# The one-hot of dst moves from VectorE (one comparison) to ScalarE (eight absolute differences and a relu)

## What is computed

```python
msg  = relu(x[src] + edge_attr @ We + be)              # 200000 x 128
aggr = segment_sum(msg, dst, num_segments=6250)
h = (1 + eps) * x + aggr
h = relu(h @ W1 + b1) @ W2 + b2
h = (h - mean(h)) * rsqrt(var(h) + 1e-5) * gamma + beta   # over the nodes
h = relu(h) + x
out = layernorm(x + h)                                  # per node
```

## Time and profile before

| | |
|---|---|
| time, median of 3 runs | 1583.06 us (1581.17 to 1585.45) |
| the profiled execution: span from its first to its last instruction | 2684.1 us; the page gives no other time of it |
| instructions in it | 58837 |
| TensorE busy | 1871.5 us, 70% of the span |
| GpSimd busy | 1154.5 us, 43% |
| VectorE busy | 991.5 us, 37% |
| ScalarE busy | 841.5 us, 31% |
| mean granted clock of TensorE | 0.809 of full speed |

### The profile page before, as it was taken

How to read it: one execution, slowest core, us unless ns; L and a number is a source line. 1 busy time by engine, 2 the same in 40 slices (tenths; PEclk the granted TensorE clock), 3 DMA queues, 4 the chain that set the end, 5 groups by cost and what they waited for, 6 DMA issues and landing times.

```text
span 2684.1 us, 58837 instructions
## 1 busy us (share of the span) xinstructions
PE 1871.5 (70%) x23395; PEld 1369.8 (51%) x23395; DVE 991.5 (37%) x3361; ACT 841.5 (31%) x1954; POOL 1154.5 (43%) x1193
## 2 busy tenths in 40 slices
PE   1776777776777777677767767767767776766776
PEld 0455555555555555555555555555555555555554
DVE  6433333333333333333333333333333333333335
ACT  3232323232332333232323323323223322322335
POOL 6444444444444444444444444434434444444421
PEclk9877788787887787788888778878778778887888
DMA  8222222232222222222222222222222222222221
GB/s 231 62 59 65 62 59 68 59 71 66 63 63 61 61 62 64 61 66 59 67 61 61 65 61 63 65 58 65 64 58 67 61 62 63 63 65 62 62 86 50
DMA packets 148455, 180.61 MB, mean 67 GB/s; under 512 B 41677, under 2 KB 128932, under 8 KB 147924
## 3 DMA queue, kind: packets, MB, share of 16 engines
q1 hardware_dynamic: 102489, 89.62, 14.0%
q0 software_dynamic: 37728, 77.31, 11.5%
q10 hardware_dynamic: 7963, 9.90, 1.2%
HBM read 170.09 MB, written 6.63 MB: 66 GB/s over the span
## 4 chain that ended last, share of the span: by engine, by line
PE 66%; issue 20%; another core or an unknown queue 8%; ACT 2%; DVE 1%; ACTq 0%; DVEq 0%
PE ps L1330 23%; PE ps L1315 15%; PE ps L1255 12%; PE ps L1269 11%; PE ps L1296 1%; PE ps L1276 1%; PE ps L1299 1%; ACT xg L694 1%; PE ps L1287 1%; PE ps L1384 1%; ACT slotS L680 0%; PE ps L1288 0%; PE ps L1394 0%; DVE lnst L1197 0%
## 5 line engine op out<-in xcount | busy, mean ns | idle before, releaser
L574 POOL DMA_INDIRECT xg<-xb,idxb x1145 | 1106.6, 966 | 1423.9 <-DVE msg L937 1068.8
L1330 PE MATMUL ps<-iota_all 128*128 128x128 bf16 x4032 | 377.8, 247 | 425.7 <-issue 291.3
L688 ACT ACTIVATE iota_all<-ps 128x384 bf16<-128x384 f32 x896 | 408.5, 489 | 775.6 <-remote 567.8
L1330 PEld LDWEIGHTS ps<-iota_all 128*128 128x128 bf16 x4032 | 290.1, 111 | 515.6 <-issue 511.5
L1022 DVE TENSOR_TENSOR accT<-accT,ps 128x64 f32 x390 | 86.5, 222 | 1138.4 <-remote 992.8
L1255 PE MATMUL ps<-we,ea 64*128 64x128 f32 x3126 | 344.2, 367 | 45.7 <-issue 45.3
L1330 PE MATMUL ps<-iota_all,hot_all 128*128 128x128 bf16 x4032 | 301.1, 229 | 102.6 <-issue 98.8
L937 DVE TENSOR_TENSOR msg<-ps,xg 128x512 f32<-128x512 f32 x390 | 262.0, 686 | 238.9 <-PE ps L1255 233.2
L1330 PEld LDWEIGHTS ps<-iota_all,hot_all 128*128 128x128 bf16 x4032 | 247.2, 102 | 172.4 <-issue 145.0
L1255 PEld LDWEIGHTS ps<-we,ea 64*128 64x128 f32 x3126 | 288.0, 261 | 80.7 <-issue 72.2
L1269 PE MATMUL ps<-msg,hot 128*64 128x128 f32 x3120 | 300.9, 352 | 6.2 <-issue 4.5
(11 more groups left out here) (135 smaller groups left out, 1113.8 us busy)
## 6 DMA issues: line engine op xcount, KB each, us to landing
ea<-in_eat SPq DMA_DIRECT2D x156, 320.0 KB
lowB<-lowD SPq DMA_DIRECT2D x128, 224.0 KB
xg<-xb,idxb POOLq DMA_INDIRECT x1145
accT<-in_xt ACTq DMA_DIRECT2D x1, 3125.0 KB
x<-in_xt ACTq DMA_DIRECT2D x1, 3125.0 KB
iota_all<-in_x ACTq DMA_DIRECT2D x1, 3080.0 KB
out<-iota_all SPq DMA_DIRECT2D x5, 512.0 KB
xb<-iota_all SPq DMA_DIRECT2D x3, 784.0 KB, 6.2
```

What stands on the lines that cost most here:

```text
L574: pool.indirect_dma_start(out=xg[0:rows, slot, j, :], out_offset=None, in_=of, in_offset=bass.IndirectOffsetOnAxis(ap=index, axis=0)).then ...
L688: act.activation(rows3[:, t, :, :].rearrange("p a h -> p (a h)"), ps_rows(k * NTILE + t), ACT.Copy)\
L1330: last = pe.matmul(found[:, e, :], sel2[set_of(k)][:, t, e * P:(e + 1) * P], rows3[:, t, a, :], start=(t == 0 and e == 0 and a == 0), stop ...
```

## The change

ScalarE gets two new functions. `offsets` writes |column - rel| into `hot`, tile by tile: eight activations Abs of 64 elements, with scale -1 and `rel`'s column of that tile as the bias (a value per partition). The last one raises a new semaphore, `s_off`. `one_hot` waits for it and turns the eight tiles in place into relu(1 - |column - rel|), one activation of 512 elements; as both are whole numbers this is 1 where they are equal and 0 elsewhere. In ScalarE's step `offsets` stands ahead of the first `clip`, `one_hot` between the two clips. VectorE's `one_hot` is gone, with its place behind the second `add_x`. The waits go along: for the ranks of a picked group, and for the `window` that last read the buffer. In the first step ScalarE waits until `rel` and the row of column numbers are written (`s_tr`). For the two tiles left over VectorE still makes the comparison, and now waits for ScalarE's last one-hot, so that `s_hot` counts in order.

```diff
+            def offsets(i, q, pair):
+                for g in (2 * q, 2 * q + 1):
+                    if special(i, g):
+                        act.wait_ge(s_rel, batch(i, SORTED.index(g)) + 1)
+                if pair >= TURN:
+                    act.wait_ge(s_win, pair - TURN + 1)
+                for m in range(2 * GROUP):
+                    t = pair * (2 * GROUP) + m
+                    last = act.activation(hot[:, q % TURN, m, :], iota, ACT.Abs, bias=rel[:, t:t + 1], scale=-1.0)
+                last.then_inc(s_off, 1)
+
+            def one_hot(q, pair):
+                act.wait_ge(s_off, pair + 1)
+                to = hot[:, q % TURN, :, :]
+                act.activation(to, to, ACT.Relu, bias=1.0, scale=-1.0).then_inc(s_hot, 1)
...
+                    if head and q == 0:
+                        act.wait_ge(s_tr, 5)
+                    offsets(i, q, pair)
                     clip(n, q, 0)
+                    one_hot(q, pair)
                     clip(n + 1, q, 1)
...
-            def one_hot(i, q, pair):
-                for g in (2 * q, 2 * q + 1):
-                    if special(i, g):
-                        dve.wait_ge(s_rel, batch(i, SORTED.index(g)) + 1)
-                if not isinstance(pair, int) or pair >= TURN:
-                    dve.wait_ge(s_win, pair - TURN + 1)
-                dve.tensor_tensor(
-                    hot[:, q % TURN, :, :],
-                    rel[:, bass.ds(pair * (2 * GROUP), 2 * GROUP)].unsqueeze(2).to_broadcast([P, 2 * GROUP, WIN]),
-                    iota.unsqueeze(1).to_broadcast([P, 2 * GROUP, WIN]), ALU.is_equal).then_inc(s_hot, 1)
...
                     add_x(i, 2 * q + 1, n + 1)
-                    one_hot(i, q, pair)
...
             dve.wait_ge(s_win, n // 2 - TURN + 1)
+            dve.wait_ge(s_hot, n // 2)
```

More of the change, by code:

```diff
@@ L306, in gine_layer_kernel @@
         s_hot = sem("s_hot")
+        s_off = sem("s_off")
         s_win = sem("s_win")
```

## The result

The changed kernel takes 1577.09 us (median of 5 runs, 1573.98 to 1577.90); the kernel before, run beside it, 1584.08 us. The ratio is 0.9947, 95% interval 0.9932 to 0.9962: 0.5% faster. The forecast was 1549 us, 2.1% faster; the direction held, the size was four times too large.

What follows compares the result with a forecast made beforehand. The prediction took GpSimd's gathers as the bound, ScalarE's added work hidden under them. 1586 less 36 us for the one-hots gave 1550 by rows, 1547 from the measured median; it predicted 1549 us, range 1515 to 1640.

Steps and rivals of the forecast that it cites:

- the 36 us for the one-hots: At gather starts: 195 VectorE one-hots each delay gathers by 0.185 us on the mean; removal gains 36 us, bounds 0 to 133.
- the stretch behind the last gather: Kernel's end: about 10 us after the last gather, then 37.9 us from the last `winS` copy; the change adds under 2 us.
- The bound: Main loop: GpSimd's gathers, 6 a step at 1.248 us, set 7.49 us a step; TensorE needs 6.93.
- The base of the sum: Whole kernel: gathers without pauses end at 1502 us, plus the end, give 1550 us; adding 36 gives 1586, near the measured 1583.
- ScalarE's path: From one `window` to the next through Abs, clips and Relu: 7.18 us a step on the mean, hidden under the gathers' 7.49.
- steps 0 and 1: Kinds of step (one pair of groups each) by q modulo 3; `window` waits 0.49 and 0.26 us there for the second clip.
- The eight Abs: ScalarE's added work in each step: 0.25 us for each Abs, 2.0 us for eight.
- TensorE's own steps: TensorE's work alone in the three kinds of step, q modulo 3: 7.46, 6.32 and 7.02 us, mean 6.93.
- (1): In the loop, ScalarE's path takes over: `window` waits for the second clip, 1632 us; dear Abs would make 1770; chance 0.26.
- (2): At gather starts: one-hots already fall where they cost nothing, so no gain, 1583 us; chance 0.15 with small changes.
- (3): In the loop: gathers are shorter in timed runs and one-hots hit harder, so more gain, near 1500 us; chance 0.04.
- (4): On ScalarE: Abs needs another function table, two loads per pair, time above 2000 us; chance 0.02.

Runs made afterwards that it cites:

- e1: The kernel before, unchanged, run and profiled a second time: one run of 1588.06 us, span 1586.0 us.
- e3: The kernel before with one gather less in each group not picked, from the second iteration on: 1481.18 us, ratio 0.9354.
- e2: The kernel before without the one-hot on any engine, VectorE only raising `s_hot`: 1563.32 us, ratio 0.9876.
- e7: The changed kernel plus the old VectorE one-hot (two SBUF operands), written to a tile nobody reads: 1593.37 us, ratio 1.0080.
- e8: The changed kernel plus a VectorE maximum of similar length (one SBUF operand) in the one-hot's old place: 1579.45 us, ratio 0.9985.
- e4: The changed kernel with one gather less in each group not picked, from the second iteration on: 1516.97 us, ratio 0.9586.
- e5: The changed kernel, but VectorE makes the one-hots of the last four steps, as before the change: 1564.09 us, ratio 0.9896.

## Why the prediction was wrong

Two terms of the sum failed: the 36 us for the one-hots were 20 to 24, and the stretch behind the last gather, carried over unchanged, grew by 13. Either alone would have left 20 to 24 us of the forecast gain of 34; together they left 7.

**The bound: right.** "I hold GpSimd's gathers to be the bound, nearly without a pause": e1 shows it, e3 proves it. It had to be inferred against the first profile, whose shares put TensorE first.

**The base of the sum: right by two errors.** Gathers without one-hots were to end at 1502 with 48 us behind them. In e2 the last one ends at 1514.5, and 48.8 us follow. The 13 us more are gathers held by other instructions of VectorE, above all the selections at L989 and L1000, which I counted at nothing: the gathers' excess in e2 sums to 19 us in the loop (16 of them at the selections), against which the 1134 gathers began 7 us sooner (at 79.53, not 86.69). So 1550 was 13 too low, and that 1550 + 36 came within 3 us of the measured time, my reason to take 36, was chance.

**The price of the one-hot: mis-sized.** 36 us were forecast; 24 show in e1's trace (and 23.9 in the gathers' rows), 20 in the time of e2. That a one-hot with its two operands in SBUF holds a gather was right (e7, e8). I let one-hots count that begin up to 0.12 us behind a gather's start; those are harmless, and with the 0.56 us that remain the sum is 24.6.

**ScalarE's path: right in kind, too long.** The waits were to be 0.49 and 0.26 us in steps 0 and 1; e4 has 0.38 and none, so 7.05 us a step, not 7.18 (so too the sign that I named, `window` waiting in steps 0 and 1, came true for step 0 alone). The eight Abs took 2.0 us, as forecast (one alone 339 ns); Relu overlapped the clip and took 0.52. As forecast, none of it shows in the loop, where 7.05 is under what the gathers need. TensorE's own steps, 7.46, 6.32 and 7.02 by the earlier trace rows, were 7.39, 6.43 and 6.95.

**The end: the step whose mechanism failed.** I carried the 48 us behind the last gather over unchanged ("No DMA and no queue is moved", the tail's cost "under 2 us once"). They became 60.4. "So the added work is hidden by the gathers" holds only while ScalarE's path has slack under them. In the last four steps it has none: the early products stand ahead of the clips there, the new work queues behind them, TensorE's `window` waits for the clip, its clock falls with the wait, and the gathers end in the midst of these steps (at 1515.0). ScalarE was busy 9.0 us of the 15.6 of the step shown, so idle time in its busy share was no slack in the order of its list. e5 gives it all back.

Together: 1584.1 - 20 + 13 = 1577, measured 1577.1. (With the 24 us of e1's trace it would be 1573; that execution was 4.8 us above the median.) Of the rivals, (1), ScalarE's path as the bound, is what happened in those four steps alone; (2), no gain, is ruled out by e2; (3), shorter gathers in the timed runs, by e1, where an undisturbed one takes 0.944 us and the next starts 0.30 later, as in the earlier trace rows; (4), another function table, by the 0.0 idle ahead of Abs. VectorE's busy time fell by 115 us (1006.6 to 891.4), not by the 133 that I named.

## What to carry to other kernels

Work moved to an engine with slack is free only in the stages where it has that slack: price it stage by stage, by where it stands in the engine's order and not by the busy share, and above all in the last stage, where nothing else is left to hide it. Where GpSimd's gathers bound a kernel, look at what runs on VectorE when a gather starts: a shorter instruction there can be worth as much as moving it away. And hold a profile's span against the timed runs before reading its shares.

## What the runs showed of the hardware

A gather that starts while a VectorE instruction with two operands in SBUF runs is held by as much as that instruction's end lies behind its own start, less 0.12 us (0.42 us for an end at 0.54; of e1's three gathers that start in a one-hot's first 0.05 us, two were not held). One that has started is not held, and does not hold VectorE to speak of: the one-hots of e1 took 681 ns in the median, 752 at the most. An addition of one operand in SBUF and one in PSUM holds no gather (`add_x`: 1.8 us over 174 gathers). Instructions on 16-bit data with one tile in SBUF do hold them. The changed kernel, VectorE and then GpSimd:

```profile
799.60 0.81 DVE L1000 TENSOR_SCALAR iota_all<-lowB,nodeu 128x896 bf16<-128x896 f16 x2
```

```profile
800.13 1.09 POOL L575 DMA_INDIRECT xg<-xb,idxb  x1 [0.30 <-issue]
```

The selection ends 0.28 us after the gather's start, and the gather takes 0.15 more than 0.94. These selections (L1000 and L1011 there) are in both kernels, and some 16 us of the loop are still theirs.
